# Up product of the routed blocks: expert weights as the stationary operand, no transposes of the inner layer

## The reference, cut to what matters

```python
xt = x.reshape(T, D)                                  # T = 2048, D = 256
probs = softmax(xt @ Wg)                              # E = 8 experts
topv, topi = top_k(probs, 2)
topv = topv / sum(topv)
cw = zeros((T, E)).at[arange(T)[:, None], topi].set(topv)
h = gelu(einsum('td,edf->tef', xt, Wu))               # F = 512
y = einsum('tef,efd->ted', h, Wd)
moe = einsum('ted,te->td', y, cw)
shared = gelu(xt @ W1) @ W2
return shared + moe
```

## Time and profile before

| what | value |
|---|---|
| median of 3 runs | 1618.93 us |
| profiled execution, time and span | 1621.81 us, 1620.5 us |
| PE busy, whole span | 1509.3 us (93%) |
| DVE, ACT, POOL busy | 1174.4, 830.1, 975.7 us |
| the 39 routed blocks | from 1431.5 to 1591.1 us |
| from the last block to the end of the span | 29.4 us |

### The profile page before, as it was taken

How to read it: one execution, slowest core, us unless ns; L and a number is a source line. 1 busy time by engine, 2 the same in 40 slices (tenths; PEclk the granted TensorE clock), 3 DMA queues, 4 the chain that set the end, 5 groups by cost and what they waited for, 6 DMA issues and landing times.

```text
span 1620.5 us, 24013 instructions
## 1 busy us (share of the span) xinstructions
PE 1509.3 (93%) x8994; PEld 1144.4 (71%) x8994; DVE 1174.4 (72%) x1905; ACT 830.1 (51%) x1191; POOL 975.7 (60%) x771
## 2 busy tenths in 40 slices
PE   4689999999999999999999999978989887999997
PEld 2478888988988988988988998734434343477776
DVE  3399889889889889889889889677676671433334
ACT  2756556656656656656656556215555565411110
POOL 1468778978978978978978998730303000034441
PEclk8899999999999999999999999979999999999999
DMA  3100110111110010010010115460324100612215
GB/s 123 52 27 28 32 47 28 35 45 47 37 50 28 30 51 28 27 53 28 27 53 30 38 58 151 79 132 12 67 52 74 31 1 20 248 46 66 66 63 172
DMA packets 36658, 92.27 MB, mean 57 GB/s; under 512 B 8128, under 2 KB 20928, under 8 KB 32192
## 3 DMA queue, kind: packets, MB, share of 16 engines
q1 hardware_dynamic: 29984, 74.73, 15.3%
q0 software_dynamic: 6048, 14.95, 3.6%
q10 hardware_dynamic: 512, 1.05, 0.4%
HBM read 64.36 MB, written 9.57 MB: 46 GB/s over the span
## 4 chain that ended last, share of the span: by engine, by line
PE 79%; DVE 13%; ACT 3%; issue 3%; DMA 1%; SPq 0%; POOL 0%; DVEq 0%; ACTq 0%; POOLq 0%
PE psum L540 25%; PE psum L521 12%; PE psum L457 6%; DVE overlay L583 4%; PE psum L1599 4%; PE psum L1584 4%; PE psum L1176 3%; DVE hst L686 3%; PE psum L1158 2%; PE psum L486 2%; PE psum L1529 2%; PE psum L1142 2%; DVE nmax L1297 2%; ACT pT L1226 2%; PE psum L1098 1%
## 5 line engine op out<-in xcount | busy, mean ns | idle before, releaser
L873 POOL TENSOR_TENSOR hst<-hst,cb 128x512 f32<-128x512 f32 x399 | 509.3, 1303 | 112.8 <-DVE hst L686 112.1
L686 DVE TENSOR_TENSOR_SCAN hst<-dA,hst,psum 128x256 f32<-128x256 f32 x399 | 277.1, 730 | 79.5 <-PE psum L540 77.7
L540 PE MATMUL psum<-filt,c_early 128*128 128x172 f32 (+1 forms) x1536 | 269.7, 312 | 9.0 <-DVE hst L686 5.9
L686 DVE TENSOR_TENSOR_SCAN hst<-dA,psum 128x256 f32<-128x256 f32 x399 | 252.8, 669 | 33.3 <-ACT dA L814 19.7
L540 PE MATMUL psum<-filt,uT 128*128 128x172 f32 (+1 forms) x1536 | 266.6, 310 | 3.4 <-DVE w_early L632 1.7
L540 PEld LDWEIGHTS psum<-filt,c_early 128*128 128x128 f32 x1536 | 233.8, 192 | 47.1 <-issue 20.8
L540 PEld LDWEIGHTS psum<-filt,uT 128*128 128x128 f32 x1536 | 230.8, 190 | 33.0 <-issue 16.0
L814 ACT ACTIVATE dA<-delta,alog 128x512 f32<-128x512 f32 x256 | 176.8, 720 | 131.1 <-DVE hst L686 99.6
L814 ACT ACTIVATE dA<-xres,alog 128x512 f32<-128x512 f32 x256 | 177.0, 719 | 126.2 <-DVE hst L686 99.5
L521 PE MATMUL psum<-ident,hst 128*128 128x128 f32 x1596 | 239.4, 273 | 0.0
L521 PEld LDWEIGHTS psum<-ident,hst 128*128 128x128 f32 x1596 | 199.3, 141 | 1.0
(11 more groups left out here) (237 smaller groups left out, 2256.0 us busy)
## 6 DMA issues: line engine op xcount, KB each, us to landing
cb<-c_rows SPq DMA_DIRECT2D x32, 1024.0 KB, 4.7
qk_first<-w_early SPq DMA_DIRECT2D x64, 64.0 KB, 2.4
qk<-part SPq DMA_DIRECT2D x64, 64.0 KB, 3.0
w_up<-up_dram SPq DMA_DIRECT2D x8, 512.0 KB, 7.4
w_down<-down_dram SPq DMA_DIRECT2D x8, 512.0 KB, 14.4
w_up<-y_choice SPq DMA_DIRECT2D x8, 512.0 KB, 7.7
qk<-part POOLq DMA_DIRECT2D x48, 64.0 KB, 5.6
qk_first<-part SPq DMA_DIRECT2D x40, 64.0 KB, 2.4
```

The lines of the kernel that those rows point to most:

```text
L540: m = pe.matmul(bk[:, :, t0:t0 + width], uT[k % 2][:, c, et * P:(et + 1) * P], filt[:, f % 2, c, n2:n2 + 2, 0:width], start=True, stop=True)
L686: dve.tensor_tensor_scan(h[:, t0:t0 + HS], dA[:, st % NDA, t0:t0 + HS], bank("v", i)[:, n * HS:(n + 1) * HS], h[:, t0 - 1:t0] if t0 else 0 ...
L873: pool.tensor_tensor(h, h, cb[:, q % 2, state_of(i)[1] % GN, :], ALU.mult).then_inc(g_done, 1)
```

## The change

`pe_up` now takes the expert's weights as the stationary operand and lets the transposed rows stream past: 8 matmuls of 128 columns (4 slices of the inner layer by 2 of the features) in place of 2 of 512. Their result has the inner layer in the partitions, which is what `pe_down` needs, so ACT's Gelu writes `ht` directly, and `pe_hidden_turn`, `dve_hidden`, the buffers `hb` and the semaphores around them are gone.

The stationary operand is not read at an address from a register: a new function `act_weights` copies the block's 128x1024 weights from `w_up` to one of NWU = 4 fixed buffers `wu`, which lie in `xn` (its contents are no longer needed then). ACT reads `block_at` for this itself. PSUM has 4 banks for the up product now instead of 2, and a few waits are written out that followed from others before: PE's down waits for `y_out2`, DVE's rows for `up_full`, ACT's Gelu for `y_full2`.

```diff
@@ buffers
-            NXB, NXT, NHT, NYB = 6, 3, 3, 4
+            NXB, NXT, NHT, NYB, NWU = 6, 3, 3, 4, 4
+            wu = xn[:].rearrange("p b k s -> p (b k s)").rearrange("p (n c) -> p n c", n=NWU)
-            hb = rest[:, NXB * D:NXB * D + 2 * F].rearrange("p (n f) -> p n f", n=2)
-            U0, H0, T0 = 0, 2, 6
+            U0, NUB, T0 = 0, 4, 6
@@ PE
-            def pe_up(j, at):
+            def pe_up(j):
                 pe.wait_ge(xt_out, j + 1)
+                pe.wait_ge(wu_set, j + 1)
                 if j == 0:
-                    pe.wait_ge(ld_up, 16 * EXPERTS)
                     pe.wait_ge(hid_act, NTR + NSH)
-                for kt in range(KD):
-                    m = pe.matmul(psum[:, U0 + j % 2, :], xt[:, j % NXT, kt, :], w_up[:, bass.ds(at + kt * F, F)], start=kt == 0, stop=kt == KD - 1)
+                if j >= NUB:
+                    pe.wait_ge(ht_out, j - NUB + 1)
+                for ft in range(FT):
+                    for kt in range(KD):
+                        m = pe.matmul(psum[:, U0 + j % NUB, ft * P:(ft + 1) * P], wu[:, j % NWU, kt * F + ft * P:kt * F + (ft + 1) * P], xt[:, j % NXT, kt, :],
+                                      start=kt == 0, stop=kt == KD - 1)
                 m.then_inc(up_full, 1)
-            def pe_hidden_turn(j):
-                pe.wait_ge(up_act, j + 1)
-                for ft in range(FT):
-                    m = pe.transpose(psum[:, H0 + j % 2, ft * P:(ft + 1) * P], hb[:, j % 2, ft * P:(ft + 1) * P], ident[:])
-                m.then_inc(ht_full, 1)
             def pe_down(j, at):
                 pe.wait_ge(ht_out, j + 1)
+                if j >= 2:
+                    pe.wait_ge(y_out2, j - 1)
@@ ACT
+            def act_weights(j):
+                at = act.value_load(block_at[0:1, j:j + 1], min_val=0, max_val=(EXPERTS - 1) * KD * F)
+                if j >= NWU:
+                    act.wait_ge(up_full, j - NWU + 1)
+                act.copy(wu[:, j % NWU, :], w_up[:, bass.ds(at, KD * F)]).then_inc(wu_set, 1)
+                act.wait_ge(blocks_set, 1)
+                act.wait_ge(ld_up, 16 * EXPERTS)
+                act_weights(0)
                 for j in range(NBLK):
+                    if j + 1 < NBLK:
+                        act_weights(j + 1)
                     act.wait_ge(up_full, j + 1)
-                    act.activation(hb[:, j % 2, :], psum[:, U0 + j % 2, :], ACT.Gelu).then_inc(up_act, 1)
+                    if j >= NHT:
+                        act.wait_ge(y_full2, j - NHT + 1)
+                    act.activation(ht[:, j % NHT], psum[:, U0 + j % NUB, :].rearrange("p (k c) -> p k c", k=FT), ACT.Gelu).then_inc(ht_out, 1)
@@ DVE
             def dve_rows(j):
                 dve.wait_ge(xt_full, j + 1)
+                if j >= NXT:
+                    dve.wait_ge(up_full, j - NXT + 1)
-            def dve_hidden(j):
-                dve.wait_ge(ht_full, j + 1)
-                dve.tensor_copy(ht[:, j % NHT], psum[:, H0 + j % 2, :].rearrange("p (k c) -> p k c", k=FT)).then_inc(ht_out, 1)
```

More of the change, by code:

```diff
@@ L1450, in build @@
             NSEND = 2 * TOPK * NT
-            posf = rest[:, NXB * D + 2 * F:NXB * D + 2 * F + TOPK * NT].rearrange("p (k t) -> p k t", k=TOPK)
+            posf = rest[:, NXB * D:NXB * D + TOPK * NT].rearrange("p (k t) -> p k t", k=TOPK)
             spare = c_early[:, (NSEND + 0) * NBLK:(NSEND + 1) * NBLK]
@@ L1475, in build @@
             NHID, OUT0, RANKS, LOGITS = 4, 4, 6, 7
-            U0, H0, T0 = 0, 2, 6
+            U0, NUB, T0 = 0, 4, 6
+            wu_set = sem("wu_set")
             NTR = B * KD
@@ L1489, in build @@
             fetched = [sem(f"fetched{n}") for n in range(NXB)]
-            xt_full, xt_out, up_full, up_act, ht_full, ht_out, y_full2, y_out2 = (
-                sem(n) for n in ("xt_full", "xt_out", "up_full", "up_act", "ht_full", "ht_out", "y_full2", "y_out2"))
+            xt_full, xt_out, up_full, ht_out, y_full2, y_out2 = (
+                sem(n) for n in ("xt_full", "xt_out", "up_full", "ht_out", "y_full2", "y_out2"))
             sent = [sem(f"sent{n}") for n in range(NYB)]
@@ L1631, in pe_ffn @@
                         at[j] = pe.value_load(block_at[0:1, j:j + 1], min_val=0, max_val=(EXPERTS - 1) * KD * F)
-                        pe_up(j, at[j])
+                        pe_up(j)
                     if j + 2 < NBLK:
                         pe_rows(j + 2)
-                    if 1 <= j <= NBLK:
-                        pe_hidden_turn(j - 1)
                     if j >= 2:
@@ L1814, in dve_ffn @@
                         dve_rows(j + 2)
-                    if 1 <= j <= NBLK:
-                        dve_hidden(j - 1)
                 for b in range(NEAR, B):
```

## The result

The changed kernel takes 1608.65 us, the median of 7 runs (1605.85 to 1615.24), the kernel before, measured beside it, 1619.76 us; the ratio is 0.993 with a 95% interval of 0.9915 to 0.9946. It is faster by 11.1 us (0.7%). Forecast were 14.4 us and 1604.5 us; the time lies inside the range of 1602.5 to 1610, but above the narrower range of 1603.3 to 1607.5 that the forecast's own mechanism gave.

What follows compares the result with a forecast made beforehand. PE alone was taken to bound the blocks; -17.2 (turns removed) + 2.3 (up product) + 0.5 (late fetches) = -14.4 us, from 1618.93 to 1604.5 us. Stated range 1602.5 to 1610, the forecast's own 1603.3 to 1607.5.

Steps and rivals of the forecast that it cites:

- The bound: Blocks, first up to last down product: PE alone sets the time, busy 159.56 of 159.60 us, 4.11 us an iteration.
- Removed from PE: PE's loop: 39 hidden turns of 0.44 us go, -17.2 us; DVE's 39 copies beside them count for nothing.
- Changed on PE: Up product: 16 records of 128 columns at 0.111 us, 1.78 in place of 1.72 us, +2.3 us over 39 blocks.
- rival 3: Up product: stationary operand loads not hidden, 190 ns in place of 111, +34.7 us, so 1654 us; chance 0.06.
- Added to ACT: ACT's weight copy of 1048 ns a block, plus register reads, hidden with some 2.5 us of cover; cost 0.
- What is late next: Fetch for the rows two iterations later: cover shrinks from 0.5 to 0.2 us, four late fetches cost +0.5 us.
- PE's own program: PE's offset read at the iteration's head and the new waits of down and DVE's rows cost nothing.
- The start: First two weight copies on ACT, before the first up product at 1431.54 us: they have room, cost nothing.
- The sum: Whole kernel: -17.2 + 2.3 + 0.5 = -14.4 us, from 1618.93 to 1604.5 us; what follows the last block keeps its length.
- rival 1: Blocks: the fetch becomes the bound, 3.89 us an iteration against PE's 3.73, +5.3 us, so 1609.3 us; chance 0.11.
- rival 2: Blocks: ACT becomes the bound with Gelu, copy and register reads taking 4.1 us, no gain, 1618.9 us; chance 0.04.

Runs made afterwards that it cites:

- idle turns: Changed kernel with four transposes, read by nobody, put back into each of the 39 iterations; 1624.13 us, ratio 1.0029 to the kernel before.
- copied_weights: Kernel before, with ACT copying each block's up weights to fixed buffers that PE streams from, all else as before; 1619.51 us, ratio 0.9997.
- copy_twice: Changed kernel with ACT copying each block's weights twice, first into columns nobody reads; 1610.47 us, ratio 0.9934 to the kernel before.

## Why the prediction was right or wrong, point by point

- **The bound.** Right. PE alone sets the blocks; its steady iteration is 3.73 us, as worked out.
- **Removed from PE, -17.2.** Right: the idle turns put 0.44 us back into every iteration.
- **Changed on PE, +2.3 at 0.111 a record.** Right: 16 records in 1.78 us. L1569 was the row to read it from. The Trainium skill's figure for sustained pairs at 128 columns ("TensorE: Matmul & The Clock Gate", section "Back-to-back issue gap") and rival 3 with it did not come: the trace has 0.111 where the estimate by that page's ratio was 0.16.
- **Added to ACT, 0.** Right, the copy takes 1045 ns where 1048 were worked out; copied_weights and copy_twice show that it is hidden.
- **What is late next, +0.5.** This is the term that was mis-sized: 3.1 us in the profiled execution, 4.15 in its repeat, 0 with more buffers. The place and the cover (0.2 us) were right; the number of late fetches and how late they are was taken over from before. Of the 33 fetches behind a send 6 were late by 0.7 to 1.1 us, and each cost 0.4 to 0.7; I had taken four at 0.3 and less. Two things were missed. The range in the earlier trace rows, 2.7 to 2.8, rests on six fetches and is not that of all, as the earlier trace rows hinted with a load that began 3.31 us after the issue. And what made them late, the loads of PE's own program, changed with the change: a third as many instructions again in a block, in a shorter iteration, and loads that fell where the fetch's rows move.
- **PE's own program, 0.** Right for PE's time, wrong for what it does to the fetch, as just said.
- **The start, 0.** Right in the profiled execution and its repeat. With more buffers, which the prediction was not about, it cost up to 4.6 us, from a cause that stays open.
- **The sum.** -17.2 + 2.6 (1.78 - 1.716 in 39 iterations) + 3.1 = -11.5 where the blocks became 11.3 shorter. The runs' medians differ by 11.1, 3.3 less than forecast; 2.6 of that are the late fetches. The rest is within what the part ahead of the blocks varies. The measured 1608.65 us is outside the forecast's own range (1603.3 to 1607.5); it was inside the stated one only because that was widened for rival 1. 0.8 of the 4.15 us between 1604.5 and 1608.65 are no fault of the sum: the kernel before had its median at 1619.76 here, not at 1618.93.
- **Rival 1**, the fetch as the bound, had the right place, but not what happened: the fetch was late one time in five or six and not each time, and the steady iteration stayed at 3.73 where the rival had 3.89. That its 1609.3 is nearest to the measured median is luck. Rivals 2 and 3 fell, rival 2 with copy_twice.

The changed kernel with eight buffers is faster than the kernel before in both comparisons, 0.9887 (0.9872 to 0.9902) and 0.9928 (0.9911 to 0.9945). Against the changed kernel only one comparison has both, 1601.30 to 1608.31 us; of these 7 us the granted clock (0.9798 to 0.9772) accounts for some 3, by the relation above, and the blocks for 4.2. What is sure is the steady iteration, and blocks of 145.2 to 146.9 us against 148.3 to 149.4 where no extra traffic runs.

## What to carry to other kernels

When a loop gets shorter, work out anew the cover of everything that runs beside it, and not only for the median: list the slowest cases of the transfer and ask what makes them slow and whether the change brings more of it. A loop with more instructions loads its own program more often, over the same DMA engines, and what a load costs hangs on where in the iteration it falls. Where an iteration's cover falls to a fraction of a microsecond, one buffer more gives it back; look at the start of the loop again after it, which here got later in most such traces. A summary of minimum, median and maximum is only as good as the number of cases in it. And before you read a difference of less than 1%, compare the granted clock of the runs on both sides.

## What the runs showed of the hardware that was not expected

- PE's program is loaded in packets of 16 KB that hold a DMA engine for 0.9 to 1.5 us; in the changed kernel one comes about every 16 us, and 12 of 66 fetches landed 0.7 to 1.4 us late by it, each by one of its 16 parts.
- A 16 KB packet of another queue does the same: rows of the fetch began as it ended, to 0.01 us, for 482 of 528 packets.
- A product whose float32 records have 128 columns, each with its own load of the stationary operand, runs at 0.111 us a record, 1.78 us for 16; the loads (192 ns each) are wholly hidden.
- 16 further instructions a block on PE's sequencer, all waits met long before, made the mean iteration 4.4 us in place of 3.8, though they use no array time.
- The code ahead of the blocks, unchanged in all kernels, ended between 1423.9 and 1435.3 us of the span, with 54.6 to 85.3 us of it at the lower granted clock.
